# Routing of the first expert layer taken into the first attention's pipeline, in four more stages

## The reference

```
x = x + tanh(g_xattn[0]) * xattn(layernorm(x), ctx)
x = x + tanh(g_ffn[0])   * experts(layernorm(x))
# experts, for each token t of the 32*256:
scores = softmax(xf @ w_router.T)            # 8 experts
expert_weights, expert_indices = top_k(scores, 2)
h = silu(xf @ w1[e]) * (xf @ w3[e]);  y[e] = h @ w2[e]
out = sum over the two chosen e of weight * y[e]
```

## Time and profile before

| | us |
|---|---|
| runs, median (lowest to highest) | 2210.8 (2208.92 to 2214.29) |
| profiled execution, its own time | 2211.83 |
| its span from first to last instruction | 2210.0 |

### The profile page before, as it was taken

One profiled execution on the slowest core, in us unless ns is written; L12 is line 12 of the kernel. 1 busy time (PEld: TensorE's weight loads), 2 busy tenths in 40 slices (PEclk: granted clock), 3 DMA queues, 4 the chain that ended last, 5 costly groups with the idle time before them and its releaser, 6 DMA issues. The chain is left out here.

```text
span 2210.0 us, 51520 instructions
## 1 busy us (share of the span) xinstructions
PE 1793.5 (81%) x16093; PEld 1493.0 (68%) x16093; DVE 1484.0 (67%) x4076; ACT 1385.6 (63%) x2601; POOL 1005.0 (45%) x1192
## 2 busy tenths in 40 slices
PE   5999999965333399999998189999999648878786
PEld 3777777745323299999998168888888536666665
DVE  4898888846443233323332289999999479999996
ACT  4898888942110144443443177777777449999997
POOL 2444444424666522222222587777776024343332
PEclk8999999985555699999999599999999969999999
DMA  3122222226442323223322445455544201121211
GB/s 105 56 86 85 85 85 85 85 84 212 144 144 81 126 85 90 87 84 90 90 85 75 91 100 124 113 110 115 122 106 99 88 29 58 60 69 57 71 57 48
DMA packets 190731, 202.52 MB, mean 92 GB/s; under 512 B 24912, under 2 KB 180304, under 8 KB 189584
## 3 DMA queue, kind: packets, MB, share of 16 engines
q1 hardware_dynamic: 166032, 166.27, 24.5%
q0 software_dynamic: 24576, 34.62, 7.7%
HBM read 126.59 MB, written 74.24 MB: 91 GB/s over the span
## 5 line engine op out<-in xcount | busy, mean ns | idle before, releaser
L1935 DVE TENSOR_TENSOR e_h<-e_s,e_ps_ab 128x256 f32<-128x256 f32 (+1 forms) x213 | 89.4, 420 | 293.8 <-ACT e_s L1761 293.8
L1726 POOL TENSOR_TENSOR e_h_lo<-e_h 128x256 bf16<-128x256 f32 (+1 forms) x213 | 130.2, 611 | 326.5 <-DVE e_h L1935 326.5
L1954 PE MATMUL e_ps_ab<-e_xt_hi,e_w_hi 128*128 128x256 bf16 (+1 forms) x852 | 233.0, 273 | 0.1
L1954 PE MATMUL e_ps_ab<-e_xt_hi,e_w_lo 128*128 128x256 bf16 (+1 forms) x852 | 232.9, 273 | 0.0
L1954 PE MATMUL e_ps_ab<-e_xt_lo,e_w_hi 128*128 128x256 bf16 (+1 forms) x852 | 232.8, 273 | 0.0
L1693 POOL DMA_INDIRECT sent_rows<-e_xn,e_slot x128 | 140.3, 1096 | 87.1 <-DVE e_seen L1868 48.8
L1761 ACT ACTIVATE e_s<-e_ps_ab 128x256 f32<-128x256 f32 (+1 forms) x213 | 81.5, 383 | 151.5 <-PE e_ps_ab L1954 151.5
L1768 ACT ACTIVATE e_yo<-e_ps_y,e_xe 128x256 f32<-128x256 f32 x142 | 59.7, 471 | 112.6 <-PE e_ps_y L1954 112.6
L2445 PE MATMUL f_ps_h<-f_qh,f_w_q 128*128 128x256 bf16 x512 | 121.6, 279 | 9.3 <-DVE f_y L2347 3.3
L1961 PE MATMUL e_ps_t<-e_ident,e_xn 128*128 128x128 f32 x128 | 33.2, 428 | 110.6 <-DVE e_xn L1808 110.6
L2178 POOL TENSOR_TENSOR f_y<-f_y,f_tmp 128x510 f32<-128x510 f32 x32 | 40.6, 1270 | 181.2 <-DVE f_y L2320 181.2
(11 more groups left out here) (438 smaller groups left out, 6639.6 us busy)
## 6 DMA issues: line engine op xcount, KB each, us to landing
e_xe<-sent_rows SPq DMA_DIRECT2D x71, 272.0 KB, 2.8
back_rows<-e_yo SPq DMA_DIRECT2D x71, 256.0 KB, 2.1
x_rows<-a_x SPq DMA_DIRECT2D x64, 256.0 KB, 2.2
a_xt<-in_xT SPq DMA_DIRECT2D x32, 256.0 KB, 2.9
a_xa<-in_x SPq DMA_DIRECT2D x32, 256.0 KB, 3.7
a_xr<-in_x SPq DMA_DIRECT2D x32, 256.0 KB, 2.8
e_xa<-x_rows SPq DMA_DIRECT2D x8, 1024.0 KB, 10.3
a_xa<-x_rows SPq DMA_DIRECT2D x32, 256.0 KB, 3.2
```

The costliest lines, as they stand in the source:

```text
L1726: nc.gpsimd.tensor_tensor(h_lo[0:k, b.par, c, :], h[0:k, b.par, c, :], h_hi[0:k, b.par, c, :], ALU.subtract).then_inc(mg.sem, 1)
L1935: nc.vector.tensor_tensor(h[0:k, b.par, c, :], s[0:k, c, :], ps_ab[0:k, c, N:2 * N], ALU.mult).then_inc(mh.sem, 1)
L1954: last = nc.tensor.matmul(to, left, right, start=(i == 0), stop=(i == len(terms) - 1))
```

## The change

The routing moves into the pipeline of the first attention. That pipeline gets ten stages in place of six, and 41 steps in place of 37. The attention itself is spread over stages 0 to 6, and stages 6 to 9 carry the routing of one batch (two tiles) at a time:

- stage 6: after `x1` is formed, its mean and variance on VectorE
- stage 7: epsilon and the root on GpSimd, the product of mean and root on VectorE
- stage 8: the normalised rows, now on ScalarE; transposes and router product on TensorE; the copy between them and the exponentials on ScalarE; the two best experts, one-hot rows, sum and reciprocal on VectorE
- stage 9: gates, rank (TensorE), slots on VectorE; the slots are stored to memory; two scatters on GpSimd, then VectorE waits for their landing (`ecol1`), rewrites the gate column, and GpSimd issues the other two

VectorE reads the logits and the ranks where TensorE left them; the base of each expert is folded into the rank products. Two copies of bf16 parts, formerly on VectorE (L439, L497), are now on ScalarE. Four of the six weight pieces are read and split in steps 0 to 10; the last two (of `w2`) are split at the start of the experts' block. A class `Shared` holds the tiles that both blocks use. The table of final places is made while tile 4 is computed, from slots read back from memory.

Step order is written anew on every queue. The core of the diff:

```diff
-            stepped(eng, step, 6, 8)
+            filled(eng, step, 10, 12, also)
@@ GpSimd
+                b = at(9)
+                if b is not None:
+                    g0.wait(gp, at(10), "paced")
+                    dve9.wait(gp, b, "eslf")
+                    nc.gpsimd.tensor_tensor(pace_g0[:, :], half[:, 0:1], half[:, 0:1], ALU.mult).then_inc(g0.sem, 1)
+                    for t in range(NT):
+                        nc.gpsimd.indirect_dma_start(sent[:, :], bass.IndirectOffsetOnAxis(ap=slot[:, b.par, t, 0:1], axis=0),
+                                                     e_xn[:, b.par, t, :], None).then_inc(e_sent[0][t][b.par], 16)
+                b = at(7)
+                if b is not None:
+                    dve6.wait(gp, b, "evar")
+                    nc.gpsimd.tensor_tensor(e_ve[:, :], e_mv[:, :, 1], eps[:, :], ALU.add).then_inc(gp7.sem, 1)
+                    act8.wait(gp, at(8), "exn")
+                    gp7.wait(gp, b, "eve")
+                    nc.gpsimd.tensor_tensor(e_rstd[:, :], e_ve[:, :], half[:, :], ALU.pow).then_inc(gp7.sem, 1)
...
@@ ScalarE
+                    for t in range(NT):
+                        last = nc.scalar.activation(e_xn[:, b.par, t, 0:D], x1[:, b.par, t, :], ACT.Identity, bias=e_nmr[:, t:t + 1], scale=e_rstd[:, t:t + 1])
...
+                    nc.scalar.activation(qx[:, :, :, 32:64], qx[:, :, :, 0:32], ACT.Copy).then_inc(act2.sem, 1)
+                    nc.scalar.activation(kx[0:S, :, 64:96], kx[0:S, :, 0:32], ACT.Copy).then_inc(act2.sem, 1)
...
+                    nc.scalar.activation(e_xf[:, :, :].rearrange("p k n -> p (k n)"), ps_d[:, :], ACT.Copy).then_inc(act8.sem, 1)
...
+                    nc.scalar.activation(e_ex[:, :, :], drop[:, :, :], ACT.Exp).then_inc(act8.sem, 1)
@@ VectorE
-                    nc.vector.tensor_copy(kx[0:S, :, 64:96], kx[0:S, :, 0:32])
-                    nc.vector.tensor_copy(qx[:, :, :, 32:64], qx[:, :, :, 0:32])
+                    landed(dve, e_sent[0][0], b)
+                    landed(dve, e_sent[0][1], b)
+                    nc.vector.tensor_copy(e_xn[:, b.par, :, D:D + 1], pair[:, b.par, :, 1:2]).then_inc(dve9.sem, 1)
@@ TensorE
+                    nc.tensor.matmul(ps_b[:, 0:NT * E], below[:, :], both[:, :, :].rearrange("p t e -> p (t e)"), start=True, stop=False)
+                    nc.tensor.matmul(ps_b[:, 0:NT * E], ones[:, :], base_part[:, :], start=False, stop=False)
+                    nc.tensor.matmul(ps_b[:, E:NT * E], ones[:, :], both[:, 0, :], start=False, stop=False)
+                    for t in range(NT):
+                        last = nc.tensor.matmul(ps_b[:, t * E:(t + 1) * E], ones[:, :], seen[:, :], start=False, stop=(t == NT - 1))
...
+                    last = transposed(ps_d, e_xn[:, b.par, :, :])
...
+                        last = product(ps_d[:, t * E:(t + 1) * E], [(e_xf[:, c, t * P:(t + 1) * P], router[:, c, :]) for c in range(KC)])
@@ weights, in `also`: SyncE loads pieces 0, 1 at step 0, 2, 3 at steps 4, 5 and 4, 5 at steps 9, 10
+                if n in (1, 2):
+                    sh.high(nc, n - 1, sh.flat[0])      # ScalarE
+                if n in (6, 7):
+                    sh.high(nc, n - 4, sh.flat[1])
+                if n in (2, 3):
+                    sh.low(nc, n - 2, sh.flat[0])       # VectorE
+                if n in (7, 8):
+                    sh.low(nc, n - 5, sh.flat[1])
@@ experts: the eight groups of the routing are gone
-            for g in groups:
-                turn_rows(g, 0)
...
+                if b.n == 4:
+                    places_()
```

More of the change, by code:

```diff
@@ new lines, in filled, with at, within @@
+def filled(eng, step, stages, fixed, also):
+    def at(n):
+        return lambda s: Batch(n - s, (n - s) // 2, (n - s) % 2) if 0 <= n - s < B else None
+    def within(batch):
+        return lambda s: batch.back(s) if s else batch
+    for n in range(fixed):
+        step(at(n))
+        also(n)
+    with eng.Fori(0, (B - fixed) // 2) as k:
+        step(within(Batch(2 * k + fixed, k + fixed // 2, 0)))
+        step(within(Batch(2 * k + fixed + 1, k + fixed // 2, 1)))
+    for n in range(B, B + stages - 1):
+        step(at(n))
@@ L183, in attention_first @@
         ch, cl = [sb(n, [P, KC, S], BF16) for n in ("ch", "cl")]
+        tick1, tick2, tick3 = [sb(f"tick{i}", [P, 1], F32) for i in (1, 2, 3)]
+        numbers = sb("numbers", [P, E], F32)
+        router = sb("router", [P, KC, E], F32)
+        below_f = sb("below_f", [P, P], F32)
+        below = sb("below", [P, P], BF16)
+        e_stats = sb("e_stats", [P, NT, 6], F32)
+        e_mv = sb("e_mv", [P, NT, 2], F32)
+        e_ve, e_rstd, e_nmr, total, e_rec = [sb(n, [P, NT], F32) for n in ("e_ve", "e_rstd", "e_nmr", "total", "e_rec")]
+        e_xf = sb("e_xf", [P, KC, N], F32)
+        top, drop, e_ex = [sb(n, [P, NT, E], F32) for n in ("top", "drop", "e_ex")]
+        base_part = sb("base_part", [P, NT * E], BF16)
+        which = sb("which", [P, NT, E], mybir.dt.uint32)
+        pair = sb("pair", [P, 2, NT, 2], F32)
+        is_k = sb("is_k", [P, 2, NT, E], F32)
+        both = sb("both", [P, NT, E], BF16)
+        found = sb("found", [P, NT, 2, E], F32)
+        more = sb("more", [P, E], F32)
         ps_a, ps_b, ps_c, ps_d = [psum(f"ps_{i}", [P, 512]) for i in "abcd"]
@@ L303, in _ @@
+            run(nc.gpsimd, step, also)
         @block.scalar
@@ new lines, in step @@
+                b = at(5)
+                if b is not None:
+                    dve5.wait(dve, b, "rec1")
+                    nc.vector.tensor_tensor(of[:, 1, :].rearrange("p (h d) -> p h d", d=HD), ps_c[:, :].rearrange("p (h e) -> p h e", e=VW)[:, :, 0:HD],
+                                            rsum[:, 1, :].unsqueeze(2).to_broadcast([P, H, HD]), ALU.mult).then_inc(dve5.sem, 1)
+                b = at(9)
+                if b is not None:
+                    landed(dve, s_st, at(11))
+                    dve9.wait(dve, b, "efound")
+                    with nc.allow_low_precision(reason="slots are whole numbers"):
+                        last = nc.vector.tensor_reduce(slot[:, b.par, :, :], found[:, :, :, :], AX_X, ALU.add)
+                    last.then_inc(dve9.sem, 1)
@@ L1522, in experts @@
-        total = sb("total", [P, T], F32)
-        rec = sb("rec", [P, T], F32)
-        pair = sb("pair", [P, 2, T, 2], F32)
-        is_k = sb("is_k", [P, 2, T, E], F32)
-        both = sb("both", [P, T, E], BF16)
-        place = sb("place", [P, T, E], F32)
-        found = sb("found", [P, T, 2, E], F32)
-        slotf = sb("slotf", [P, GR, T, 2], F32)
-        slot = sb("slot", [P, 2, T, 2], I32)
-        more = sb("more", [P, E], F32)
-        seen = sb("seen", [P, E], BF16)
+        ident, bases, ends, tri, iota, starts, ones, seen = sh.ident, sh.bases, sh.ends, sh.tri, sh.iota, sh.starts, sh.ones, sh.seen
```

1273 lines of the change are left out of this document (621 added, 652 removed).

## The result

| | before | after |
|---|---|---|
| median of four runs (lowest to highest), us | 2211.4 (2208.9 to 2214.3) | 2146.3 (2142.4 to 2148.8) |
| profiled execution: span, us | 2210.0 | 2143.0 |

The ratio is 0.9704, 95% interval 0.9684 to 0.9724: 65 us faster, where 131 were forecast. The forecast was 2080 us with a range of 2040 to 2130; the time lies outside it.

What follows compares the result with a forecast made beforehand. Three nearly full engines bound the first attention, a chain the routing; a 16.3 us step (+89.0), four more steps (+28) and weights (+5), with 131.7 gained by the first tile and 1 lost after, gave 2080 us (2040 to 2130).

Steps and rivals of the forecast that it cites:

- The added wait: VectorE's second-column copy awaits both first scatters' landing: 4.0 us, hidden behind some 5.5 us of work; upper end 1 us.
- VectorE's work: Attention step: VectorE goes from 12.2 to 15.7 us, 24 small operations at 0.13 adding 3.1; 16.1 with collisions.
- the port: Attention step: collisions with GpSimd lengthen some eight VectorE operations, 0 to 2 us, taken as 0.4.
- the statistics: Attention step: two statistics of 128x256 on VectorE, 0.34 us each, add 0.7 us.
- Steady steps: Attention: period 16.3 us (14.5 to 18.5) instead of 13.52, over 32 batches +89.0 us.
- Weights: Attention: four weight pieces fall into steps that aren't full, +5 us of 12.3.
- Fill and drain: Attention's partly filled steps: four more steps at 7 us each, +28 us (0 to 54).
- closing: From the attention's end to the first expert tile: 22.0 us (17 to 30).
- the rest of the kernel: After the first expert tile: the table of places in tile 4 costs 0 to 2 us, taken as 1.
- GpSimd's ring: Rival, attention step: scatters cost 1.57 us, GpSimd reaches 17.2, landing late, period 17.5; 2118 us, chance 0.21.
- The starved scatters: Rival, attention step: scatters take 3.50 + 0.30 us beside a never idle VectorE, 208 us more; 2288 us, chance 0.05.
- Engines only: Rival, attention step: small operations cost 0.08, nothing collides, TensorE sets period 15.4; 2051 us, chance 0.20.

Runs made afterwards that it cites:

- e2: Changed kernel with SyncE waiting for both first scatters' landings before it issues its bunch of transfers: 2076.3 us, ratio 0.9382 to the kernel before.
- e5: Changed kernel with SyncE waiting for the first scatters' landings only ahead of the x and context loads: 2122.2 us, ratio 0.9588.
- e1: Changed kernel with the second gate copied to a tile of its own, so nothing waits for the landing within a step; computation partly left out: 2062.1 us.
- e7: e2 with eight more small VectorE reductions of 128x16 per step: 2079.1 us, ratio 0.9404.
- e6: e2 with splits of the third and fourth weight piece moved to steps 34 to 36, loads of the fifth and sixth to 36 and 37: 2075.3 us.
- e8: e2 with half of the router product left out on TensorE: 2074.2 us, ratio 0.9377.

## Why the prediction failed

The forecast for the attention was 122.0 us more; it took 186.1 (669.2 - 483.1). The 64.1 us of the miss, term by term:

**The added wait, the step that failed.** The prediction had 4.0 us from the slots to the landing and 5.5 us of VectorE's work between, "I count the wait as hidden". The work was there: 5.7 us, from 403.27 to 408.97 in the step above. The scatters cost what was said. The landing, taken from scatters of the routing stage, is 5.4 and not 2.5 us, past the upper end of 4.4 too, so that the wait is 1.75 us and not nothing, and above the 1 us of the range. e2 and e5 show the cause: SyncE's bunch. SyncE's new order was there to be read, and the prediction didn't ask what SyncE issues within the same 3 us. The price is larger than the wait: e1 and e2 take 2.8 us off the step where the wait is 1.75. The rest is 0.6 us more busy time of VectorE (15.28 against 14.64), since with the shift the match stands still beside GpSimd, and 0.4 us of waiting at L625.

**VectorE's work, wrong the other way.** The sum was 15.7 plus 0.4 for the port and 0.2 of slack. Without the wait the step is 14.9, VectorE busy for 14.64: 2.48 more than before and not 3.5 to 3.9. By e7 a small operation costs 0.07 and not 0.13; at that price, an estimate for all 24, they come to 1.7 instead of 3.1. The two copies that left are 0.28 and 0.22 us in the trace before and not 0.16 each, 0.5 in all. The meetings with GpSimd cost 0.7 more than before in e2 (cast 0.4, sum 0.3, first copy of the gate 0.3, less the 0.3 that the cast lost before), where 0.4 stood, and about 1.5 in the changed kernel. With the 0.7 for the statistics that gives 2.6, near the 2.48.

**Steady steps: 36 us of the miss.** 26 gaps at 17.68 and not 16.3. Against e2's 14.94 the late landing costs 26 x 2.74 = 71 us of it, and VectorE's work, priced too dear, gives 35 back.

**Weights: 4 us.** The six early gaps lie 9.0 us over the steady ones, forecast 5. With the shorter step of e2 they lie 19.5 over them, and the pieces that e6 moves away cost 16. The end of 12.3 that the prediction named was closer there.

**Fill and drain: 24 us.** Forecast 28 for the four added steps and 2.78 for each of the six batches outside the 26 gaps, 44.7 in all. It took 68.9: the first closing 4.3 later, the last five gaps 33.9 more than before, and 30.7 from the last closing to the last scatter. The last five gaps are most of it: 15.0 us each where they took 8.3 before, 20 us beyond the 2.78 each of the forecast. VectorE waits 13.7 us for landings in them; but e2, where it waits 5, still takes 27.7 more than before, so most of this isn't the late landing. What it is, beyond steps that carry routing where they had run empty, no run takes apart. The 30.7 is near the 28, with this in each of the last three steps:

```profile
649.39 0.17 DVE L747 COPY k_xn<-a_pair 128x2 f32<-128x2 f32 x1 [4.66 <-DMA sent_rows<-k_xn,k_slot]
...
658.25 0.17 DVE L747 COPY k_xn<-a_pair 128x2 f32<-128x2 f32 x1 [4.59 <-DMA sent_rows<-k_xn,k_slot]
...
665.93 0.17 DVE L747 COPY k_xn<-a_pair 128x2 f32<-128x2 f32 x1 [4.54 <-DMA sent_rows<-k_xn,k_slot]
```

There VectorE has nothing to cover two scatters and a landing, in e2 as well (4.6 each). Counted from the start of the last closing the stretch takes 31.4 us, in e2 31.1, and without that wait, in e1, 26.0.

**Luck in the total.** With the wait hidden, as in e2, the time is 2076, 4 us from the forecast, but by errors that cancel: 35 us too much for the steady steps against 15 too little for the weights and 17 too little for fill and drain.

**What held.** ScalarE under VectorE; TensorE at 14.7 us per step in e2, the lower end of its 14.7 to 15.2, but level with VectorE and not below it; GpSimd far from full; the scatters at 1.26 from start to start (1.29 measured); closing 21.5 us for 22.0; the rest of the kernel + 1.2 for + 1; the clock at 1.00 in the steady steps of e1 and e2.

**The rivals.** GpSimd's ring (2118 us, 0.21) named the sign that came true, a wait of L747 in every step, and a period of 17.5 for 17.7. Its mechanism didn't: the scatters take 0.98 and not 1.57 us, and GpSimd is idle for a third of the step. The starved scatters (2288 us) never came; by the prediction's own terms their threshold is (20.4 - 7.6) / 4 = 3.2 us with the gap, 2.9 without it. The Trainium skill, "SBUF — State Buffer", section "Who interferes with whom", has VectorE and GpSimd exclude one another for a whole instruction, in the kinds of instruction that it names. The trace agrees for the match and the sum, which have two inputs in SBUF. But the prediction gave the starved scatters 208 us and the other direction, VectorE's short instructions beside GpSimd's long ones, 0.4 us per step at a quarter of a microsecond each; in this kernel it is the second that costs, 1.5 us at one match. "Engines only" (2051 us, 0.20) came nearest to the step without the wait, 15.4 for 14.9 in e1, but named TensorE as what sets it, against which e8 speaks, and had the forecast's fill and drain.

## What to carry to other kernels

A wait for a transfer must be priced with the transfers that other queues have on the engines in the same few microseconds; read every queue's issues around it. If the wait can't move, move the bulk transfers behind it: two lines on SyncE were worth 3% here, as their data had slack. And before a small two-input or cast instruction of VectorE is placed, look what GpSimd runs at that moment: here its price was often not its size but the rest of GpSimd's instruction (the cast 0.66 us for 0.16), or of two (the sum 2.76 for 0.14).
